# Row maxima of the attention scores from two 64-row products placed side by side in TensorE, and a new order of a head's slot

## What is computed

```python
q = jnp.einsum('bse,hed->bhsd', x, Wq) + bq[None, :, None, :]
k = jnp.einsum('bse,hed->bhsd', x, Wk) + bk[None, :, None, :]
v = jnp.einsum('bse,hed->bhsd', x, Wv) + bv[None, :, None, :]
scores = jnp.einsum('bhsd,bhtd->bhst', q, k) / jnp.sqrt(jnp.float32(DH))
scores = jnp.where(causal[None, None, :, :], scores, -jnp.inf)
attn = jax.nn.softmax(scores, axis=-1)
out = jnp.einsum('bhst,bhtd->bhsd', attn, v)
...
x = x + attn_a(layernorm(x)); x = x + ffn(layernorm(x))
x = x + attn_b(layernorm(x)); x = x + ffn(layernorm(x))
```

## Time and profile before

| | us |
|---|---|
| median of 3 runs | 575.68 (575.47 to 575.82) |
| the profiled execution, its own time | 579.0 |
| its span, first to last instruction | 577.0 |
| PE, PEld busy | 528.2, 369.8 |
| DVE, ACT, POOL busy | 444.7, 468.5, 455.8 |
| mean granted TensorE clock | 0.988 |

### The profile page before, as it was taken

The page is one execution under the profiler, slowest core; times in us unless marked ns, Lnnn a source line. Parts: engine busy times, 40 slices in busy tenths (PEclk is TensorE's granted clock), DMA queues, the critical chain, the costliest instruction groups (busy, mean ns, idle before and its releaser), DMA issues.

```text
span 577.0 us, 17876 instructions
## 1 busy us (share of the span) xinstructions
PE 528.2 (92%) x6844; PEld 369.8 (64%) x6844; DVE 444.7 (77%) x1383; ACT 468.5 (81%) x923; POOL 455.8 (79%) x446
## 2 busy tenths in 40 slices
PE   4688999899999999999999999997988998788886
PEld 3445666566676667666766667664788795546664
DVE  5588888788888888888888888887776575689822
ACT  3659889889988999899989999889873869473983
POOL 5658899678888888888888888896965956564995
PEclk9989999999999999999999999999989999899999
DMA  9423334232433333423334243358108000000001
GB/s 230 113 56 72 85 86 111 56 94 58 119 84 94 93 76 102 104 74 96 80 104 110 56 121 77 100 141 319 39 38 292 2 3 2 1 1 2 1 20 55
DMA packets 36435, 48.54 MB, mean 84 GB/s; under 512 B 10728, under 2 KB 17792, under 8 KB 36352
## 3 DMA queue, kind: packets, MB, share of 16 engines
q1 hardware_dynamic: 34240, 46.88, 29.6%
q10 hardware_dynamic: 2112, 0.54, 0.4%
HBM read 12.79 MB, written 9.44 MB: 39 GB/s over the span
## 4 chain that ended last, share of the span: by engine, by line
PE 65%; ACT 10%; DVE 9%; issue 8%; POOL 7%; DMA 1%; POOLq 0%; ACTq 0%; DVEq 0%
PE psum L555 9%; PE psum L611 9%; PE psum L612 9%; PE psum L509 6%; PE psum L511 6%; PE psum L510 6%; PE psum L591 5%; PE psum L593 5%; PE psum L592 5%; PE psum L614 2%; ACT xn L1130 2%; ACT p_hl L1202 2%; POOL h_lo L2077 2%; POOL p_hlb L2084 2%; POOL p_hl L2004 2%
## 5 line engine op out<-in xcount | busy, mean ns | idle before, releaser
L2004 POOL TENSOR_TENSOR p_hl<-p,p_hl 128x512 f16<-128x512 f32 x288 | 327.4, 1162 | 54.0 <-ACT p_hl L1202 50.6
L1481 DVE CUSTOM_DVE_ANT_0 max_junk<-psum,mask_s 128x1024 bf16<-128x1024 f32 (+7 forms) x256 | 190.2, 753 | 32.0 <-issue 31.8
L1201 ACT ACTIVATE p<-psum 128x512 f32<-128x512 f32 x288 | 178.2, 619 | 16.4 <-PE psum L614 14.1
L1202 ACT ACTIVATE p_hl<-psum 128x512 f16<-128x512 f32 x288 | 179.6, 624 | 0.0
L591 PE MATMUL psum<-v_all,p_hl 128*128 128x65 f16 x1152 | 125.5, 193 | 1.7 <-POOL p_hl L2004 1.7
L611 PE MATMUL psum<-q_hl,k_hh 128*128 128x512 f16 (+3 forms) x384 | 125.1, 326 | 1.4 <-ACT p_hl L1202 1.4
L592 PE MATMUL psum<-v_all,p_hl 128*128 128x64 f16 x1152 | 125.6, 193 | 0.0
L593 PE MATMUL psum<-v_all,p_hl 128*128 128x65 f16 x1152 | 125.2, 194 | 0.0
L612 PE MATMUL psum<-q_hm,k_l 128*128 128x512 f16 (+3 forms) x384 | 121.8, 326 | 0.0
L591 PEld LDWEIGHTS psum<-v_all,p_hl 128*128 128x128 f16 x1152 | 107.4, 98 | 16.7 <-POOL p_hl L2004 1.8
L592 PEld LDWEIGHTS psum<-v_all,p_hl 128*128 128x128 f16 x1152 | 106.7, 97 | 4.9
(11 more groups left out here) (205 smaller groups left out, 1109.1 us busy)
## 6 DMA issues: line engine op xcount, KB each, us to landing
k_hh<-st_hi SPq DMA_DIRECT2D x64, 128.0 KB, 2.3
o_scratch<-o_sb SPq DMA_DIRECT2D x16, 512.0 KB, 2.6
o_in<-o_scratch SPq DMA_DIRECT2D x4, 2048.0 KB, 10.5
k_l<-st_lo SPq DMA_DIRECT2D x32, 128.0 KB, 2.3
q_hl<-st_hi SPq DMA_DIRECT2D x32, 128.0 KB, 2.3
q_hl<-st_lo SPq DMA_DIRECT2D x32, 128.0 KB, 2.3
q_hm<-st_hi SPq DMA_DIRECT2D x32, 128.0 KB, 2.3
x_sb<-in_L_attn_a_x SPq DMA_DIRECT2D x4, 256.0 KB, 3.7
```

The source lines that it names most:

```text
L1201: nc.scalar.activation(p32[:, ring_at(u, r), :], src, ACT.Exp, scale=SCALE_A).then_inc(exp_done, 1)
L1202: nc.scalar.activation(p_hl[:, u % 2, 0, BANK * r:BANK * (r + 1)], src, ACT.Exp, scale=SCALE_A).then_inc(phi_done, 1)
L1481: nc.vector.tensor_tensor_reduce(out=max_junk[:, n % 2, 0:cols], in0=max_banks(v, j, 0, cols), in1=mask_s[:, S - cols:S], scale=1.0, scala ...
L2004: nc.gpsimd.tensor_tensor(p_hl[:, u % 2, 1, cols], p32[:, ring_at(u, r), :], p_hl[:, u % 2, 0, cols], ALU.subtract)\
```

## The change

The maxima's products use the high halves alone, 64 rows instead of 128. Each product is placed either in the upper rows (q_hl and k_hh rows 0 to 63) or in the lower ones (q_hm and k_hh rows 64 to 127, which both hold high halves now), and they are issued in pairs, one in each half: for blocks 7 to 4 the first 512 columns and the rest; then block 3 with block 2, and block 1 with block 0. The columns written to PSUM and what DVE reduces stay the same. To have q's high halves in the lower rows, q_hm and k_l1 swap their halves: the DMAs, the memsets and `max_rows` change their partitions, and their sizes stay. The order within a slot is new on PE, ACT and DVE.

```diff
-                sp.dma_start(k_l1[0:DH, s, :], st_lo[rows, 0, :]).then_inc(k_moved[par], 16)
+                sp.dma_start(k_l1[DH:P, s, :], st_lo[rows, 0, :]).then_inc(k_moved[par], 16)
...
-                sp.dma_start(q_hm[0:DH, s, :], st_hi[rows, 1, :]).then_inc(q_moved[par], 16)
+                sp.dma_start(q_hm[DH:P, s, :], st_hi[rows, 1, :]).then_inc(q_moved[par], 16)
...
                 if v:
-                    pe.wait_ge(max_done, QT * v + (n - max_alone(j)))
+                    pe.wait_ge(max_done, QT * v + n)
                 elif n >= 2:
-                    pe.wait_ge(max_done, n - 1)
-                cols = P * (j + 1)
-                for c0 in range(0, cols, BANK):
-                    c1 = min(c0 + BANK, cols)
-                    last = nc.tensor.matmul(max_banks(v, j, c0, c1), q_hl[:, s, P * j:P * (j + 1)], k_hh[:, s, c0:c1],
-                                            start=True, stop=True)
-                last.then_inc(max_full, 1)
+                    pe.wait_ge(max_done, n - 1 + int(j < CT))
+                if j >= CT:
+                    nc.tensor.matmul(max_banks(v, j, 0, BANK), q_hl[0:DH, s, P * j:P * (j + 1)], k_hh[0:DH, s, 0:BANK], start=True, stop=True)
+                    nc.tensor.matmul(max_banks(v, j, BANK, P * (j + 1)), q_hm[DH:P, s, P * j:P * (j + 1)], k_hh[DH:P, s, BANK:P * (j + 1)],
+                                     start=True, stop=True).then_inc(max_full, 1)
+                else:
+                    i = j - 1
+                    nc.tensor.matmul(max_banks(v, j, 0, P * (j + 1)), q_hl[0:DH, s, P * j:P * (j + 1)], k_hh[0:DH, s, 0:P * (j + 1)],
+                                     start=True, stop=True).then_inc(max_full, 1)
+                    nc.tensor.matmul(max_banks(v, i, 0, P * (i + 1)), q_hm[DH:P, s, P * i:P * (i + 1)], k_hh[DH:P, s, 0:P * (i + 1)],
+                                     start=True, stop=True).then_inc(max_full, 1)
...
@@ def pe_slot(u):
+                maximum(0)
                 products(0)
                 products(1)
-                maximum(0)
                 project(0)
                 scores(u, 0)
                 scores(u, 1)
                 maximum(1)
                 products(2)
                 scores(u, 2)
                 project(1)
                 maximum(2)
                 products(3)
                 scores(u, 3)
                 scores(u, 4)
                 maximum(3)
                 scores(u, 5)
                 value_unit()
                 maximum(4)
-                maximum(5)
                 products(4)
+                scores(u, 6)
                 products(5)
-                scores(u, 6)
+                products(6)
                 maximum(6)
-                products(6)
+                products(7)
                 if late_chunk(u) is not None:
                     pe.wait_ge(v_lo_done, units_after(u))
                     turn_chunk(late_chunk(u))
+                products(8)
                 scores(u, 7)
-                maximum(7)
-                products(7)
-                products(8)
                 rows()
                 scores(u, 8)
...
@@ head 0, ahead of the slots
             for n in range(QT):
-                max_tile(0, n)
+                if n not in (5, 7):
+                    max_tile(0, n)
...
@@ def act_slot(u):
                 project(0)
+                if late_chunk(u, 2) is not None:
+                    late_norm(late_chunk(u, 2))
                 exponentials(u, 0)
                 exponentials(u, 1)
+                project(1)
                 exponentials(u, 2)
-                project(1)
-                if late_chunk(u, 2) is not None:
-                    late_norm(late_chunk(u, 2))
                 exponentials(u, 3)
-                exponentials(u, 4)
                 if unit_in(u) is not None:
                     value_high(unit_in(u))
+                if late_chunk(u) is not None:
+                    chunk_high(late_chunk(u))
+                exponentials(u, 4)
                 exponentials(u, 5)
                 exponentials(u, 6)
-                if late_chunk(u) is not None:
-                    chunk_high(late_chunk(u))
                 exponentials(u, 7)
                 exponentials(u, 8)
...
@@ def max_rows(v), def dve_slot(u):
-                nc.vector.tensor_tensor(q_hm[DH:DH + QT, set_of(v), :].rearrange("p (j q) -> p j q", j=QT),
+                nc.vector.tensor_tensor(q_hm[0:QT, set_of(v), :].rearrange("p (j q) -> p j q", j=QT),
...
                 maximum(0)
-                if late_chunk(u, -1) is not None:
-                    first_stats(late_chunk(u, -1))
                 project(0)
...
                 maximum(6)
+                if late_chunk(u, -1) is not None:
+                    first_stats(late_chunk(u, -1))
                 maximum(7)
+                outputs(1)
                 if u + 1 < HEADS:
                     max_rows(u + 1)
-                outputs(1)
```

More of the change, by code:

```diff
@@ L1966, in _ @@
             pool.wait_ge(rstd_done, 2)
-            nc.gpsimd.memset(k_l1[DH:P, :, :].bitcast(F32), 0.0).then_inc(kl_zeroed, 1)
+            nc.gpsimd.memset(k_l1[0:DH, :, :].bitcast(F32), 0.0).then_inc(kl_zeroed, 1)
             pool.wait_ge(fourths_ready, 2)
@@ L1979, in _ @@
             pool.wait_ge(diag_ready, 1)
-            nc.gpsimd.memset(q_hm[DH:P, :, :].bitcast(F32), 0.0).then_inc(qm_zeroed, 1)
+            nc.gpsimd.memset(q_hm[0:DH, :, :].bitcast(F32), 0.0).then_inc(qm_zeroed, 1)
             pool.wait_ge(norm_done, 3)
@@ L1985, in _ @@
             pool.wait_ge(pow_done, 2)
-            nc.gpsimd.memset(k_l1[DH:DH + QT, :, :].bitcast(I32), ROW_BITS).then_inc(rows_ready, 1)
+            nc.gpsimd.memset(k_l1[0:QT, :, :].bitcast(I32), ROW_BITS).then_inc(rows_ready, 1)
             pool.wait_ge(rows_ready, 1)
```

## The result

The changed kernel takes 591.97 us in the median of four runs (590.76 to 592.83), against 575.75 us for the kernel before on the same chips. The ratio of the runs is 1.0257, with a 95% interval of 1.0218 to 1.0295. It is **slower** by 2.6%, some 15 us (12.6 to 17.0 by the interval). The forecast was 563.5 us with a range of 554 to 580.

The account below looks back on a forecast made before the run. PE's own work was taken to bound the slots: 10.3 us saved in 22 steady slots and 1.9 in others, less 0.3 for head 0, made 11.9 off 575.7, or 563.8; forecast 563.5 us, range 554 to 580.

Parts of the forecast that it names:

- changing between 128 and 64 rows: On PE, twelve times a slot: taken to cost 0, within bounds of 0 and 0.165 us.
- the row nearest in kind: Trace row of the turned maxima on PE (L570), eight columns wide between full products, read as showing no pause.
- second rival: Every change of rows empties PE's array: 590 us at 0.08 a change, 622 at 0.165; chance 0.15.
- the 0.22 wait at scores(5): PE waits 0.22 us a slot for unit 2's bank, as ACT now takes project(1) ahead of unit 2.
- the 0.12 for second starts: On PE, a pair's second matmul starts late for its own weights and issue: 0.02 us a pair, 0.12 a slot.
- the 0.06 for gaps: Saving per PE slot from rounding and small gaps, of which 0.08 us, half of the old 0.14, was kept.
- Side by side: A pair on PE costs only its wider product: maxima 1.19 us instead of 1.94, 0.75 less a slot; chance 0.70.
- The sum of PE's slot: PE's work per steady slot, added from start-to-start distances: 11.61 us, plus 0.14 rounding and small gaps, for 11.75.
- DVE's narrow cover, outputs(1) ahead of max_rows: DVE's 0.56 us outputs(1) stays covered by PE's work, with 0.08 us to spare where it was 0.29.
- Nothing from the order elsewhere, slots 1 to 6 a little faster: Outside steady slots: slots 0 to 2 gain about 0.3 us each, 3 gains 0.47, 5 some 0.5, 4 and 6 about 0.
- The gain that the rows promised: Steady slots on PE fall from 11.75 to 11.28 us, 0.47 less, or 10.3 us over 22 slots.
- Theory A: Theory of the follow-up experiments: each change between 128 and 64 rows costs PE some 0.10 us.

Follow-up runs that it names:

- the order alone: The changed kernel with its new slot order, but the maxima's products kept as the earlier 128-row ones; 581.74 us, ratio 1.0077 to the kernel before.
- the added ones: Kernel before with four 64-row by 64-column products added to each slot, into unread columns; 603.60 us, against 580.15 us for the control with 128-row products.
- the 32-wide form: Kernel before with four 128-row products, only 32 columns of weights wide, added to each slot; 602.04 us, ratio 1.0420.
- the upper rows alone: The changed kernel with all twelve 64-row products in the upper rows, so none runs beside another; 616.71 us, ratio 1.0683 to the kernel before.
- pairs in the old order: Kernel before with the change's 64-row pairs and swapped halves, all else in its old place; 589.90 us, ratio 1.0227.

## Why the prediction was wrong

**The step that failed** is the one on changing between 128 and 64 rows: "I take 0, the value of the row nearest in kind". Measured it is 0.097 us a change, twelve times a slot: 1.16 us paid for 0.75 saved. By the prediction's own second rival the change turns at 0.04; at 0.097 that rival gives 1.16 - 0.47 = 0.69 a slot, 0.69 x 31 = 21, 597 us. Two terms of it were too dark: the 0.22 wait at scores(5) and the 0.12 for second starts were not there. Without them, and without the 0.06 for gaps, it is 1.16 - 0.75 = 0.41 a slot, 0.41 x 31 = 12.7, 588 us; the order's own loss, 4.1 us in the run of the order alone, brings it to about the 592 measured. The prediction had put that at nothing, so it is a second, smaller step that failed. The rival had 0.15 of the chance and the range stopped short of it.

The row was nearest in what it changes (the shape of the tile) but not in the kind of operation: it is float32 and a transpose, the pairs are float16 products (and the added ones bfloat16). The added forms show that the row did not carry over; whether type, operation or width is the reason stays open. It was not a matter of rows against width: the 32-wide form pays as the 64-row one does. The prediction also called the row's 0.11 what 128 float32 columns take; at full width they take 0.14. The Trainium skill's "TensorEngine Tiling (Array Packing)", Tiling Modes, Key Properties, has a change of mode drain the engine. For 16-bit products the trace agrees in effect, by rows and by width, at 0.10 us each way; at the float32 transpose of 8 columns no such loss shows.

**Side by side.** Right, and fully: starts 0.00 to 0.01 apart, 0.76 us between the pairs and the same products in the upper rows alone. The 0.02 a pair for the second's weights was not needed. "TensorE: Matmul & The Clock Gate", Part 3, in the Trainium skill gives 4 ns between such starts; the trace has no finer step than 0.01 and agrees.

**The sum of PE's slot.** Right. With it, 11.74 for the order alone gives 11.74 - 0.75 + 12 x 0.097 = 12.15; the change has 12.13.

**The wait at scores(5).** Not there in the steady slots: from 130 to 388 us PE waited for ACT once, for 0.2 us, and with the order alone, at 11.74 a slot, not at all between 142 and 400 us. That the stretched slot gives ACT the time is likely, not shown; no run has a slot of 11.3 us, where the wait was forecast.

**DVE's narrow cover, outputs(1) ahead of max_rows.** It held in the steady slot: 12.13 in the new order beside 12.22 in the old with the same pairs.

**Nothing from the order elsewhere, slots 1 to 6 a little faster.** Wrong in sign: 78.9 us for slots 1 to 6 with the order alone, against 76.8, and 92.2 against 88.4 with slot 0. Part of it (slots 4 and 5, 0.9 and 0.4 us) comes with ACT's project(1) ahead of unit 2. Slot 0's 1.7 us goes mostly with the granted clock: at the same mean clock the new order's slot 0 is longer by 0.1 to 0.5 us (12.19 to 12.38 beside 11.85 to 12.09 at 0.86; 13.29 and 13.32 beside 13.17 at 0.74). What makes the rest of slots 3 to 6 longer is not settled.

**The gain that the rows promised** therefore went, in the steady slot, wholly into changes of the tile: 0.75 saved, 1.16 paid, 0.41 lost; measured 0.38 to 0.47. Theory A's number holds in four unlike kernels: 0.096 (upper rows only), 0.095 (the change against the order alone), 0.102 (pairs in the old order), 0.097 (added products).

## What to carry to other kernels

Two 64-row products side by side save the narrower one's columns, but a pair in the midst of 128-row work pays two changes of the tile, some 0.2 us, about one full 512-column matmul: by these numbers it can pay off only where several pairs follow one another with no full product between, which no run here tried. Here a pair fills both banks of the maxima and the next waits until DVE has read them, so the six stay apart. Before a cost is taken from the nearest row, ask in what that row differs from the new operation besides the property in question (here type, kind and width), and put the rest of the range where the answer is unknown. And multiply a small unknown by how often it comes: at twelve a slot, 0.04 us decided the sign.

## What the runs showed that was not expected

- A change of the tile, by rows or by width, costs 16-bit products 0.09 to 0.10 us each way, and the next weights are not loaded ahead across it (weight loads at 204.01 and 204.33, and at 202.75 and 202.88 around an added product, start with their own matmuls, in the stream around them one matmul earlier).
- A float32 transpose 8 columns wide pays none of it (steps 0.03 and 0.11), has its weights loaded ahead (204.25 and 204.28), and is shorter than the full-width one (0.14).
- A single edit on an engine that is not the bound, ACT's project(1) one unit earlier, lengthened slots 4 and 5 by 1.4 us together in its profile and left the steady slot as it was (11.74).
- The sum of the slots between two profiles moves by up to 2.6 us with the clock granted in slot 0 (10.69 us at 1.00, 13.32 at 0.74), in either order of the slot; it can hide or feign an edit's effect.
